# Applying a per-head inverse to two heads at once: block-diagonal stationary of 128x16 columns, results turned by products with slices of the identity

## The reference

```
h = layernorm(x) * (1 + ca) + sa ;  xn = layernorm(h) * g + b
q, k, v = heads(xn @ Wq), heads(xn @ Wk), heads(xn @ Wv)      # chunks [128, 64]
G = Kc.T @ Kc + 1e-4 * I                                      # 64 x 64
W = solve(G, Kc.T @ Vc)
U = I[:, :8]
for _ in range(2):
    U, _ = qr(W @ U)
S = 0.9 * S + U @ (U.T @ W)
out = 0.125 * (Qc @ S)
x = x + ga * (x' + concat(out) @ Wo)       # then a feed-forward block with FP4 quantisation:
x = x + gb * ffn(layernorm(x) * (1 + cb) + sb)
```

## Time and profile before

| what | value |
|---|---|
| median of 3 runs | 1582.87 us (1582.31 to 1584.79) |
| the profiled execution's own time | 1578.29 us |
| its span, first to last instruction | 1576.5 us |
| mean granted TensorE clock | 0.811 |
| PE busy, instructions | 994.5 us (63%), 19646 |
| PEld busy | 792.3 us (50%) |
| DVE busy | 1293.8 us (82%) |
| ACT busy | 650.0 us (41%) |
| POOL busy | 225.0 us (14%) |
| chain that ended last, by engine | PE 46%, DVE 26%, issue 10%, ACT 5% |
| matmul groups of L933 (`products`) | 4096 with `ya` and 2048 with `yb` |
| matmuls of L948 (the transposes) | 384 |

### The profile page before, as it was taken

One profiled execution on the slowest core, in us unless ns is written; L12 is line 12 of the kernel. 1 busy time (PEld: TensorE's weight loads), 2 busy tenths in 40 slices (PEclk: granted clock), 3 DMA queues, 4 the chain that ended last, 5 costly groups with the idle time before them and its releaser, 6 DMA issues.

```text
span 1576.5 us, 48154 instructions
## 1 busy us (share of the span) xinstructions
PE 994.5 (63%) x19646; PEld 792.3 (50%) x19646; DVE 1293.8 (82%) x3840; ACT 650.0 (41%) x1366; POOL 225.0 (14%) x149
## 2 busy tenths in 40 slices
PE   1344910596276789777789876773474832997165
PEld 1333510464265667666667665662463721776144
DVE  5884589859998779899779799889489789889677
ACT  3563610264143456543456543452242520664032
POOL 3551001101102001302001302001500000001200
PEclk9555965698589899988889988897687975999577
DMA  2555100011000001110001110012220200210000
GB/s 73 174 174 181 30 25 0 2 29 41 1 4 3 4 10 44 39 59 4 4 6 47 32 53 3 4 37 81 66 72 1 72 16 0 78 31 24 9 14 23
DMA packets 52109, 61.94 MB, mean 39 GB/s; under 512 B 4048, under 2 KB 32416, under 8 KB 51888
## 3 DMA queue, kind: packets, MB, share of 16 engines
q1 hardware_dynamic: 51888, 58.84, 12.1%
HBM read 38.31 MB, written 20.51 MB: 37 GB/s over the span
## 4 chain that ended last, share of the span: by engine, by line
PE 46%; DVE 26%; issue 10%; ACT 5%; POOL 2%; DMA 1%; POOLq 0%; SPq 0%; DVEq 0%; ACTq 0%
PE a_bank L688 6%; DVE a_blocks L1561 5%; DVE a_outer L1553 5%; PE a_bank L826 5%; PE a_bank L759 4%; PE a_bank L933 4%; PE a_bank L816 3%; PE a_bank L832 3%; PE a_bank L702 3%; PE a_bank L914 3%; PE a_bank L948 3%; PE a_bank L884 2%; PE a_bank L777 2%; PE a_bank L787 2%; ACT a_work L1076 1%
## 5 line engine op out<-in xcount | busy, mean ns | idle before, releaser
L1553 DVE TENSOR_TENSOR a_outer<-a_blocks 128x512 f32<-128x512 f32 (+19 forms) x608 | 308.9, 541 | 11.7
L1561 DVE TENSOR_TENSOR a_blocks<-a_blocks,a_outer 128x512 f32<-128x512 f32 (+19 forms) x608 | 303.7, 532 | 0.8
L1076 ACT ACTIVATE a_work<-a_bank 128x512 f32<-128x512 f32 (+1 forms) x193 | 110.3, 602 | 215.7 <-PE a_bank L798 174.3
L1466 POOL TENSOR_TENSOR a_root<-a_recip,a_half 128x32 f32<-128x32 f32 (+2 forms) x24 | 91.6, 3819 | 699.0 <-DVEq L1576 692.2
L798 PE MATMUL a_bank<-a_ident,a_blocks 128*128 128x128 f32 x256 | 36.5, 311 | 167.2 <-DVE a_blocks L1612 165.6
L1076 ACT ACTIVATE a_solve<-a_bank 128x512 f32<-128x512 f32 (+2 forms) x184 | 87.9, 523 | 108.1 <-PE a_bank L832 50.2
L688 PE MATMUL a_bank<-a_wk,a_cg 128*128 128x512 f32 x256 | 121.2, 619 | 0.0
L798 PEld LDWEIGHTS a_bank<-a_ident,a_blocks 128*128 128x128 f32 x256 | 35.4, 201 | 167.9 <-DVE a_blocks L1612 125.9
L1076 ACT ACTIVATE a_xb<-a_bank 128x512 f32<-128x512 f32 x112 | 63.5, 597 | 90.6 <-PE a_bank L933 54.1
L1076 ACT ACTIVATE a_scaled<-a_bank 128x512 f32<-128x512 f32 (+1 forms) x130 | 65.4, 530 | 78.0 <-PE a_bank L816 68.1
L816 PE MATMUL a_bank<-a_solve,a_work 32*32 32x64 f32 x4096 | 58.2, 247 | 62.3 <-issue 49.0
(11 more groups left out here) (197 smaller groups left out, 2236.1 us busy)
## 6 DMA issues: line engine op xcount, KB each, us to landing
f_x<-in_L_attn_x SPq DMA_DIRECT2D x16, 256.0 KB, 3.1
s_xnt<-f_xt SPq DMA_DIRECT2D x16, 256.0 KB, 2.1
s_c<-f_cm SPq DMA_DIRECT2D x16, 256.0 KB, 2.3
s_base<-f_base SPq DMA_DIRECT2D x16, 256.0 KB, 2.8
a_cg<-s_c SPq DMA_DIRECT2D x16, 256.0 KB, 2.8
a_cc<-s_c SPq DMA_DIRECT2D x16, 256.0 KB, 3.9
a_xnt<-s_xnt SPq DMA_DIRECT2D x16, 256.0 KB, 3.9
a_base_in<-s_base SPq DMA_DIRECT2D x13, 256.0 KB, 2.6
```

The source lines that it names most:

```text
L1076: nc.scalar.activation(out, view, ACT.Copy, scale=scale).then_inc(emptied, 1)
L1466: nc.gpsimd.tensor_tensor(root[:, :, a:b], recip[:, :, a:b], half[:, :, a:b], ALU.pow).then_inc(roots_ok, 1)
L1553: return ch.inc(V.tensor_tensor(product, bcast(column, 2, area.shape[2]), bcast(row, 3, area.shape[3]), ALU.mult))
L1561: return ch.inc(V.tensor_tensor(area, area, product, ALU.add))
```

## The change

The vectors of two heads lie in one tile `yz` of [128, NQ, 2, 8], in which slot s holds data only on the partitions of head s and zeros on the others. Its 128x16 columns for one pair of problems are a block diagonal, so one product applies the inverse of both heads. Its output has 16 rows in each 32-row column group, and one bank takes what two took. `via` then holds, for each place, a stationary operand of 128x64, and a product with `pick[s]` (32 columns of the identity) brings head s's 8 vectors of 4 column groups to the partitions of head s. All of a step's results fit into 256 columns of one bank, and ACT moves them in one activation. ACT writes `yz` by two activations of 64 partitions where it wrote `ya` by one of 128. `yz` is cleared once by DVE at the start of the main pass, and the scratch of the compiler's dynamic DMAs is set to 8192, which makes room for the larger tile. `APPLY_UNITS` falls from 16 to 8, so the woven stages are interleaved differently.

```diff
-        ya, yb = (sb(n, [P, NQ, R]) for n in ("ya", "yb"))
+        yz, yb = sb("yz", [P, NQ, 2, R]), sb("yb", [P, NQ, R])
+        pick = [ident[:].rearrange("p (c z r) -> p z c r", c=4, r=R)[:, s] for s in range(2)]
...
+        def turned(via, k):
+            return via.rearrange("p t d -> p (t d)")[:, BANK * k:BANK * k + BANK].rearrange("p (i d) -> p i d", d=DH)
...
-            def apply_inverse(self, src, mark, via):
+            def apply_inverse(self, mark, via):
...
                 def products(k):
-                    two = self.u.fill(2, apart=True)
+                    bank = self.u.fill(apart=True)
                     for i in range(8):
                         for c in range(4):
-                            for s in range(2):
-                                q = 32 * k + 8 * c + i
-                                last = nc.tensor.matmul(two[s][32 * c:32 * c + R, i * DH:(i + 1) * DH], src[rows(s, None), q, :],
-                                                        pair[rows(s, None), q, :], start=True, stop=True)
-                    last.then_inc(filled, 2)
+                            q = 32 * k + 8 * c + i
+                            last = nc.tensor.matmul(bank[32 * c:32 * c + 2 * R, i * DH:(i + 1) * DH], yz[:, q].rearrange("p z r -> p (z r)"),
+                                                    pair[:, q, :], start=True, stop=True)
+                    self.done(last)
...
-                    for half in range(2):
-                        bank = self.u.fill()
-                        for i in range(4):
-                            last = nc.tensor.transpose(bank[:, i * P:(i + 1) * P], via[:, 8 * (k % 2) + 4 * half + i], ident[:])
-                        self.done(last)
+                    bank = self.u.fill()
+                    for i in range(8):
+                        for s in range(2):
+                            last = nc.tensor.matmul(bank[rows(s, None), i * 4 * R:(i + 1) * 4 * R].rearrange("p (c r) -> p c r", r=R), turned(via, k)[:, i],
+                                                    pick[s], start=True, stop=True)
+                    self.done(last)
...
-            def heads(self, dst):
+            def heads(self, dst=None):
...
+                    if dst is None:
+                        for s in range(2):
+                            last = nc.scalar.activation(of(yz[rows(s, None), :, s]), view[rows(s, None)], ACT.Copy)
+                        last.then_inc(emptied, 1)
...
-                    for s in range(2):
-                        bank = self.u.empty()
-                        self.move(via[:, 8 * (k % 2):8 * (k % 2) + 8, s * DH:(s + 1) * DH], bank[:].rearrange("p (i d) -> p i d", d=DH))
+                    bank = self.u.empty()
+                    self.move(turned(via, k), bank[:].rearrange("p (i d) -> p i d", d=DH))
...
-                    for half in range(2):
-                        bank = self.u.empty()
-                        self.move(dst[:, 32 * k:32 * k + 32].rearrange("p (c i) r -> p i c r", c=4)[:, 4 * half:4 * half + 4],
-                                  bank[:].rearrange("p (i c z) -> p i c z", i=4, c=4)[:, :, :, 0:R])
+                    bank = self.u.empty()
+                    self.move(yb[:, 32 * k:32 * k + 32].rearrange("p (c i) r -> p i c r", c=4),
+                              bank[:, 0:8 * 4 * R].rearrange("p (i c r) -> p i c r", i=8, c=4))
...
-        APPLY_UNITS = 4 * (NQ // 32)
+        APPLY_UNITS = 2 * (NQ // 32)
...
+                ch.link(V.memset(yz[:], 0.0))
+                dve.sem_inc(yz_ok, 1)
...
-    nc = bacc.Bacc("TRN2", target_bir_lowering=False, num_devices=1)
+    nc = bacc.Bacc("TRN2", target_bir_lowering=False, num_devices=1, dynamic_dma_scratch_size=8192)
```

47 lines of the change are left out of this document (28 added, 19 removed).

## The result

| | before | after |
|---|---|---|
| median, same chip | 1582.32 us (1574.91 to 1584.79, 7 runs) | 1572.53 us (1567.79 to 1578.04, 7 runs) |
| ratio | | 0.9948, 95% interval 0.9924 to 0.9971 |
| span of the profiled execution | 1576.5 us | 1570.7 us |

The change is faster by about 0.5%, 8 to 10 us, where 29.4 were forecast. 1572.53 lies just above the range of 1540 to 1572. The two profiled executions differ by only 5.9 us, as that of the kernel before was 4 us under its median.

The account below looks back on a forecast made before the run. PE and ACT were taken to bound the loop in two stages, with DVE close behind. Gains of 25.0 us in the loop and 4.4 in the tail sum to 29.4, giving a median of 1553 us, range 1540 to 1572.

Parts of the forecast that it names:

- The step that failed: Loop, `lead_return` and `schur` up to DVE's next schur factor: assumed to take 42.5 us, as before the change.
- the terms of 9.0, 7.0 and 1.0: Gains in us from the shorter subspace in the loop's first, second and third iterations.
- a cooled PE costs at most 0.4: Stage behind a lead factor after long idle time: took 42.9 us against 42.5, so cooling costs at most 0.4 us.
- The count of 127: PE in an application: it pauses for its next instruction block every 127 matmuls, 3.87 us a block.
- 13 to 14 were forecast: Sign: length in us of one application outside a woven stage, 18.2 before.
- Array: One application step on PE: 64 products in 0.99 us, 32 turning products in 0.97, together 0.41 us less than before.
- Rival 2: Full-row products don't run side by side in four column groups; 6 us slower, 1589 us; chance 0.12.
- Woven stage: Each woven stage in the loop gains 4.0 us: 1.6 from four shorter steps, the rest from a 2.33 us pause removed.
- Tail: Last group's woven stages: 2.8 us gained ahead of `gate_up(3)`'s end and 1.6 in `output`, together 4.4.
- Rival 1: Pauses stay, following bursts and not instruction count; 1569.5 us; chance 0.22 including what lies between it and the forecast.
- PE's idle time at `lead_return`: Sign: PE would stand idle there, waiting for DVE's lead factor; no size given.
- 9, 20 and 25: Sign: how many us earlier the loop's schur factors would start.

Follow-up runs that it names:

- e8: Kernel after with 128 idle transposes ahead of PE's wait for the lead factor in `lead_return`; 1578.9 us, ratio 0.9979 to the kernel before.
- e6: Kernel after with every turning product of an application issued twice, same result; 1580.43 us, ratio 0.9993 to the kernel before.
- e9: Kernel after with 16 idle transposes ahead of PE's wait for the lead factor; 1561.47 us, ratio 0.9859 to the kernel before.
- e13: Kernel after with 16 idle transposes ahead of PE's wait and the last group's old weaving order; 1549.71 us, ratio 0.985 to the kernel before.
- e2: Kernel after with 64 bare semaphore increments on PE's queue ahead of its wait for the lead factor; 1578.7 us, ratio 0.9994 to the kernel before.
- e10: Kernel after with 96 idle transposes ahead of PE's wait for the lead factor; 1566.21 us in one execution.
- e11: Kernel after with 96 idle transposes ahead of PE's wait and the last group's old weaving order; 1559.64 us, ratio 0.9847 to the kernel before.
- e1: Kernel after with 64 idle transposes ahead of PE's wait for the lead factor; 1563.75 us, ratio 0.9907 to the kernel before.
- e7: Kernel after with 64 idle transposes ahead of PE's wait and the last group's old weaving order; 1566.54 us, ratio 0.9905 to the kernel before.
- e5: Kernel after without POOL's multiplication by ga in `combine`, so the output lacks the gate; 1553.91 us, ratio 0.983 to the kernel before.
- e4: Kernel after with the last group's two woven stages interleaved in the old order; 1564.0 us, ratio 0.9905 to the kernel before.

## Why the prediction was wrong

**The step that failed** is "I assume 42.5 us again, now from the later of the lead factor's end and the subspace's end". It measured 43.2 us behind lead factor 0, and 48.9, 49.5 and 44.2 in the loop, and with it went the terms of 9.0, 7.0 and 1.0. The argument that "a cooled PE costs at most 0.4" rested on the length of a single stage behind a long idle time (42.9), and that length hid the cost: from 290.57 to 333.43 PE was busy for 35.6 us and idle for 7.2, where the stage from 519.40 had 33.2 and 10.2. The busy time was already 2.4 us longer, and shorter pauses made up for it. Two things came together:

- *The clock.* In the kernel after PE is busy some 3 us longer for the same matmuls, at a granted clock that is lower by 0.03 to 0.05. PE waits where it never waited before, and the transposes directly behind (3.5 us before, 5.0 to 6.3 after) are slow for that reason: in e8 and e6, with the wait filled, they are at 3.5 again in the first two groups. That part is 2.2 us in the mean. The clock later in the stage is not governed by the wait alone, as e9 against e13 shows, and why it differs is open.
- *The extra pause.* A second pause in the first row of products makes the stage's idle time 11.8 and 12.1 us, 1.6 and 3.3 more than before. It stays when the wait is filled by work in the application (e6), and is gone in all ten stages in which transposes or increments moved the boundary away from product 111 (e2, e9, e10, e11, e13). So position is needed for it. It is not enough: in e8 the boundary is at the same place and the pause is gone, and in e1 and e7, one program in the loop, it is in one iteration and not in the other. What else decides is open.

Of the 23.5 us between forecast and profiles, the three stages behind the wait are 13.1, the tail 7.5, the first row of the table, which can't be told from chance, 1.6, and the woven stages 1.3.

**Blocks.** The count of 127 held (64 products, 32 turning products and 31 products lie between the pauses ahead of 499.45 and of 503.43), and the application did get shorter, 18.2 to 11.0 us where 13 to 14 were forecast. The Trainium skill (Runtime: NRT & Kernel Launch, Instruction fetch mechanics) has the crossing between blocks mostly hidden; the rows above, with 2.34 and 1.61 us in one row of products, disagree. The forecast used the blocks for the changed code alone and left the pauses of the unchanged code behind it where they were, though it removes 160 matmuls ahead of them in each application.

**Array.** 0.99 us was forecast for 64 products and 1.02 measured; 0.97 and 1.05 for 32 turning ones. Rival 2 is out. The rule beside it in the Trainium skill (TensorE: Matmul & The Clock Gate, Part 3, The mechanism), that a load overlaps with matmuls in flight only where the row groups differ, is not borne out for this form: all loads here use every row, and it is 15.9 ns from product to product with a new load each. `heads` cost 1.04 us for 0.9 forecast.

**Woven stage.** The term was 4.0 us each; 2.3 and 4.4 came. PE's saving was enough for all of the 4.37 and 6.49 us of idle time. What took 2.2 us back each time is POOL's collision with DVE, which the forecast did not have: the two operations at the factor's end got 1.07 us longer each, and e5 gives one of them back. The term counted a wait as free to remove in which `combine` had been running.

**Tail.** -4.4 forecast, +3.1 measured. In e4, e9, e11 and e13 it is -3.0 to -3.7, which looks like the term. But the kernel before with 16 or 32 transposes has a tail of 542.8 or 544.0, as short as the best of the changed kernel (543.0 to 543.7), so no run shows that the change itself shortens the tail, and the term of 4.4 stays unshown. Either the old order or 16 transposes take the loss away, and both together take no more (543.4, 543.2, 543.0). The order cost 6.4 us only at this position (3.0, 2.2 and 0.2 at the others), so I can't call it the order's own price. In PE's rows the loss goes with busy time (329.65 us against 323.45 in e13); what causes it is open.

**Rivals.** None had this mechanism. Rival 1's time of 1569.5 is near by accident, since it has the pauses stay in the application, where most of them went. The direction, faster with a chance of 0.85, held. The ratios of 0.9859, 0.9847 and 0.985 (e9, e11, e13) say that the change can be worth 1.5%, some 24 of the 29.4 us, of which it kept 8 to 10 as it stood. The same 16 transposes bring the kernel before nothing (1.0009), so this is not what padding alone gives.

**The profile.** Of the signs that were forecast, PE's idle time at `lead_return` and the pace of the products came. DVE no longer waited ahead of any `orthogonalise`, where 2 to 3 us were forecast ahead of the first, as the application was shorter than forecast. The schur factors started only 3.4, 5.4 and 9.0 us earlier instead of 9, 20 and 25. A slip of reading is that DVE stands idle 7 times in the earlier trace rows: the rows and the list behind it have eight. No term hangs on it.

## What to carry over

When work is taken off the critical path, the engine that did it will wait, and the stage behind the wait is then not the one that was measured without a wait: price it at the lower clock, here 2.2 us for its first 32 transposes, and look at what used to run in the idle time that goes. Compare the busy and the idle time of two stages separately, because equal lengths can hide a slower clock behind shorter pauses. Where an engine pauses for its next block of instructions, any change in instruction count moves the boundaries of all code behind it, and padding in a function counts once for each place where it stands in the program. Before a verdict of half a per cent is believed, a few transposes of padding at an idle place are worth trying, here 0.9948 against 0.9859. Versions with 16 or 96 of them (e9, e11, e13) beat both kernels by that test.

## What was not expected of the hardware

- 128 bare semaphore increments on PE took 18.66 us and 64 took 9.03, about 0.14 us each.
- A DVE operation of 128x512 takes 1.75 us instead of 0.68 while POOL runs a tensor_tensor beside it, one of 128x1024 2.30 instead of 1.23. Of POOL's own two beside them, the multiplication stayed at 1.29 us, and the addition took 2.12 instead of 1.30.
- The same program took 44.7 and 41.5 us for one stage in two executions on two chips. PE was busy for 35.4 and 32.5 us of it at a granted clock of 0.83 and 0.90, and idle for 9.3 and 9.0.
